# Per-row score maxima: turned by matmuls that read each column 64 times over, in place of a spread copy and a transpose

## The chip, the cores and the metric

The kernel runs on one core of a Trainium2 chip. The metric is the device time of one execution in microseconds (us). The engines are PE (TensorE, with its weight loads shown apart as PEld), DVE (VectorE), ACT (ScalarE), POOL (GpSimd) and SP (SyncE, which here only issues DMAs). Each runs its own list of instructions in order, and waits on semaphores for the others.

## The reference

One transformer block, float32, batch 2, 2048 positions, width 256, 16 heads of 64, hidden width 768:

```
hn = layernorm(h) * gamma + beta
q, k, v = hn @ Wq + bq, hn @ Wk + bk, hn @ Wv + bv      # 16 heads of 64
q, k = rope(q), rope(k)
attn = softmax(where(causal, q @ k.T * 64**-0.5, -inf))
x = layernorm(h + (attn @ v) @ Wo + bo + h)
out = layernorm(x + (silu(x @ Wg) * (x @ Wu)) @ Wd + x) # integer weights times 1/127
```

## The kernel before

The work on attention is cut into 16 pairs of heads (8 pairs for each of 2 batches; `it` counts them from 0). The two heads of a pair lie in the two halves of the 128 partitions (`halves`), 64 rows each. A pair has 16 query tiles of 128 rows and 4 blocks of 512 queries, and its scores are made transposed, keys on the partitions: 40 units of 128 keys by up to 512 queries (`UNITS`). Two units make a group, and every engine runs through the same 20 groups, `g` from 0 to 19, in the same order (`pair`, written once for each engine).

The softmax subtracts each row's maximum. The maxima are made ahead of the scores, from a coarser product: `maxima` on PE writes a query tile against up to 512 keys, for both heads, into the two banks of `m_ps`; `maximum` on DVE reduces it along the keys (L833) and, for tiles with several pieces, reduces the pieces once more (L836). So the negated maximum of query row p of tile t, head a, ends in `mc[p, block, t, a]`: one number per partition, a column. `m_ps` is not doubled: PE's next `maxima` waits until DVE has reduced the last.

The scores need these maxima along the free axis, on the partitions of the head's half, because they are added by one more product: `ones_r` (64 rows of ones) times `aux` (L1211) adds the sum over the half's 64 rows of `aux` to every score of a query. Before the change this goes in three steps. `spread` on DVE copies 8 columns of `mc` (4 tiles, 2 heads) into `mz`, a buffer of zeros, at column 0 and column 64 of each tile (L847). `turn_maxima` on PE transposes the four tiles of `mz` into `x_ps` (L1222), so that row 0 and row 64 hold the maxima and the other rows are zero. `shifts` on ACT copies `x_ps` to `aux` (L575).

There is one such turn for each block, called M0 to M3: M1 in group 1, M2 in group 5, M3 in group 11, and M0 of the next pair in group 19. The table `XUSE` has them, since the one bank `x_ps` is shared with the projections of the next pair's q and k ("Q0", "K0", ...), with v ("V0", ...) and with the row sums ("R0", ...). `shared_free` makes PE wait until the last user has left the bank: before M2 that is K0, before M3 it is Q2, and both are left by DVE (`products`: L860 writes `qr`, L864 writes `qc`). The rope needs the halves of `qr` swapped: SP issues four DMAs for it (L385, `rot<-qr`), and then DVE adds (`turned_sum`, L871); ACT rounds (L569) and DVE takes the rest (`piece_lo`, L876).

In a turn's group PE runs: one `maxima`; the scores of two units (L1205 to L1215); the turn; `weigh` of the group before (the probabilities times v, L1239). DVE runs: the copy (`spread`); the sums' transpose (group 1) or the two `products` (groups 5 and 11); the maximum of this group; then the rest. POOL adds up the probabilities (`acc`, L542) all the time.

L1239 and L1222 differ in how PE's array is cut. L1239 has 128 rows by 64 columns of weights, one half for each head, and the two halves run side by side; the trace shows each plain float32 product as two records. L1222 uses all 128 by 128, and a transpose is one record.

Of the kernel before, what the change touches and what calls it, by code (L numbers as in the profile page):

```python
# [8 lines left out]
F32 = mybir.dt.float32  # L9
# [4 lines left out]
P = 128  # L14
BATCH, SEQ, DM = 2, 2048, 256
HEADS, DK = 16, 64
# [3 lines left out]
TT = SEQ // P  # L20
# [3 lines left out]
TG = 4  # L24
GROUPS = TT // TG
NB = 512
BLOCKS = SEQ // NB
# [11 lines left out]
NM = len(MUNITS)  # L39
GU = 2  # L40
NG = NU // GU
# [21 lines left out]
TURN_M = {g: int(x[1]) for g, x in XUSE.items() if x[0] == "M"}  # L63
# [38 lines left out]
def postln_block_kernel(nc, h, gamma, beta, wqkv, bqk, bv, wo, bo, wgate_t, wup_t, wdown_t,  # L102
                        cos, sin, ident, masks, attn, hn_far, v_far, out):
    h, out = h.rearrange("b s d -> (b s) d"), out.rearrange("b s d -> (b s) d")
    with ExitStack() as ctx:
        def sb(name, shape, dt):
            return ctx.enter_context(nc.sbuf_tensor(name, shape, dt))

        def sem(name):
            return ctx.enter_context(nc.semaphore(name))  # L110
# [6 lines left out]
        id_f = sb("id_f", [P, P], F32)  # L117
        mask_b = sb("mask_b", [P, 4, P], BF16)
        id_b = sb("id_b", [P, DK], BF16)
        ones_r = sb("ones_r", [P, P], F32R)  # L120
# [6 lines left out]
        b_v = sb("b_v", [P, OC], F32)  # L127
        mz = sb("mz", [P, TG, P], F32)
        mc = sb("mc", [P, BLOCKS, TG, 2], F32)
# [77 lines left out]
        with ExitStack() as ctx_ps:  # L207
# [3 lines left out]
            x_ps = ctx_ps.enter_context(nc.psum_tensor("x_ps", [P, NB], F32))  # L211
# [48 lines left out]
        maxed = sem("maxed")  # L260
        m_rows = sem("m_rows")
        mz_done = sem("mz_done")
        m_turned = sem("m_turned")
# [10 lines left out]
        normed = sem("normed")  # L274
# [30 lines left out]
        out_stored = sem("out_stored")  # L305

        FIRST, MIDDLE, SWITCH, LAST = "first", "middle", "switch", "last"
# [472 lines left out]
        def _(dve):  # L780
            nc.vector.memset(mz[:, :, :], 0.0).then_inc(normed, 1)
            nc.vector.memset(ones_f[:, :], 1.0).then_inc(o_stored, 16)
            nc.vector.memset(ones_r[:, :].bitcast(F32), 1.0).then_inc(out_stored, 16)
            nc.vector.memset(r_i[:, :], 0.0).then_inc(tile_done, 1)
# [42 lines left out]
            def maximum(n, m):  # L827
# [6 lines left out]
                if parts > 1 and c == parts - 1:  # L834
                    dve.wait_ge(maxed, n * NM + (m + 1))
                    nc.vector.tensor_reduce(mc[:, t // TG, t % TG, :], mpart[:, t % 2, :, 0:parts],  # L836
                                            AX.X, ALU.min).then_inc(m_rows, 1)

            def spread(n, blk, first=False):

                if blk == 0:
                    dve.wait_ge(maxed, n * NM + TG)
                else:
                    dve.wait_ge(m_rows, n * (TT - TG) + TG * blk)
                if not first:
                    dve.wait_ge(m_turned, n * BLOCKS + blk)
                nc.vector.tensor_copy(mz[:, :, :].rearrange("p t (a d) -> p t a d", a=2)[:, :, :, 0], mc[:, blk, :, :])\  # L847
                  .then_inc(mz_done, 1)

# [60 lines left out]
            def pair(kind, it, par, pr, batch):  # L910
                for g in range(NG):
                    turns = g in TURN_M and (g != NG - 1 or kind is not LAST)
                    if turns and kind is not FIRST:
                        spread(it + 1 if g == NG - 1 else it, TURN_M[g])
                    ended = EVICTED.get(g) if g != 1 or kind is not FIRST else None
# [6 lines left out]
                    for m in ms[:late]:  # L922
                        maximum(it, m) if m < NM else maximum(it + 1, m - NM)
                    if turns and kind is FIRST:
                        spread(it + 1 if g == NG - 1 else it, TURN_M[g])
                    if g - 2 in PIECE and kind is not LAST:
# [81 lines left out]
            remainders(1)  # L1008
            spread(0, 0, first=True)
            unturned(3)  # L1010
# [126 lines left out]
        def _(pe):  # L1137
# [6 lines left out]
            halves = (slice(0, DK), slice(DK, P))  # L1144
# [74 lines left out]
            def turn_maxima(n, blk):  # L1219
                pe.wait_ge(mz_done, n * BLOCKS + (blk + 1))  # L1220
                for t in range(TG):
                    last = nc.tensor.transpose(x_ps[:, t * P:(t + 1) * P], mz[:, t, :], id_f[:, :])  # L1222
                last.then_inc(m_turned, 1)
# [254 lines left out]
```

## Time and profile before

| | us |
|---|---|
| median of 3 runs | 2232.11 (2231.62 to 2236.57) |
| profiled execution, its own time | 2229.82 |
| profiled execution, span | 2228.0 |
| PE busy | 2070.0 (93%) |
| DVE busy | 1597.6 (72%) |
| POOL busy | 1391.7 (62%) |
| ACT busy | 906.6 (41%) |

The busy times are unions over the span. The times in the rows further down count from the start of the span. The 16 pairs run from about 70 us to 1850 us; the input's normalization and first projections lie before, the output projection and the feed-forward part behind.

### The profile page before, as it was taken

How to read it: one execution, taken by the hardware profiler on the slowest of the kernel's cores; microseconds unless marked ns; L12 is line 12 of the kernel's file. 1: busy time of each engine (PE TensorE's matmuls, PEld its weight loads, DVE VectorE, ACT ScalarE, POOL GpSimd, SP SyncE). 2: the span in 40 equal slices, each digit the busy share in tenths (PEclk: the TensorE clock that was granted, in tenths of full speed). 3: DMA queues.
4: the chain of work that ended last, by engine and by line, in shares of the span. 5: the costliest groups of instructions: out<-in, count | busy, mean ns of one | idle time of the engine just before them, and what ended most of it. 6: DMA issues, size and time to landing. Idle time of an engine off the chain costs nothing.

```text
span 2228.0 us, 37497 instructions
## 1 busy us (share of the span) xinstructions
PE 2070.0 (93%) x14720; PEld 1287.2 (58%) x14720; DVE 1597.6 (72%) x2262; ACT 906.6 (41%) x1245; POOL 1391.7 (62%) x1204
## 2 busy tenths in 40 slices
PE   6779999999999989999999999999999989889997
PEld 5445555555555545555555555555555545789996
DVE  8576878686878776767777777778787763556654
ACT  4424443444444434434343434343434345434342
POOL 1457777777787866677767777878787879000000
PEclk9899999999999999999999999999999999999999
DMA  6311212121202122122111212121112131231300
GB/s 223 119 30 38 62 39 62 39 62 39 58 25 68 42 68 72 45 65 63 48 53 43 58 43 58 43 58 34 48 34 58 29 119 48 67 104 57 112 10 29
DMA packets 116149, 132.16 MB, mean 59 GB/s; under 512 B 15248, under 2 KB 71184, under 8 KB 115728
## 3 DMA queue, kind: packets, MB, share of 16 engines
q1 hardware_dynamic: 115984, 129.92, 19.5%
q8 instruction: 109, 1.79, 0.3%
q14 instruction: 56, 0.46, 0.1%
HBM read 56.47 MB, written 39.85 MB: 43 GB/s over the span
## 4 chain that ended last, share of the span: by engine, by line
PE 60%; DVE 24%; DMA 5%; SPq 4%; issue 4%; ACT 1%; POOL 1%; ACTq 0%; DVEq 0%
PE o_ps L1239 13%; DVE mpart L833 9%; PE m_ps L1184 7%; DMA rot<-qr 5%; PE s_ps L1205 4%; SPq L385 4%; PE s_ps L1209 4%; PE s_ps L1207 4%; PE s_ps L1211 4%; PE x_ps L1139 3%; DVE qr L860 3%; PE x_ps L1246 3%; DVE qc L871 2%; PE gu_ps L1139 2%; PE gu_ps L1140 2%
## 5 line engine op out<-in xcount | busy, mean ns | idle before, releaser
L542 POOL TENSOR_TENSOR acc<-acc,pt 128x512 f32<-128x512 f32 (+3 forms) x1024 | 1195.8, 1200 | 228.0 <-ACT pt L591 228.0
L591 ACT ACTIVATE pt<-s_ps 128x1024 f32<-128x1024 f32 (+3 forms) x640 | 544.8, 895 | 704.8 <-PE s_ps L1211 342.4
L833 DVE TENSOR_REDUCE mpart<-m_ps 128x2 f32<-128x1024 f32 (+2 forms) x576 | 624.9, 1085 | 288.2 <-PE m_ps L1184 215.7
L1239 PE MATMUL o_ps<-pt,v 128*64 128x512 f32 (+3 forms) x2560 | 547.5, 549 | 0.0
L1184 PE MATMUL m_ps<-qk 64*128 64x512 f32 (+3 forms) x1280 | 290.0, 449 | 85.0 <-DVE mpart L833 73.7
L1184 PEld LDWEIGHTS m_ps<-qk 64*128 64x128 f32 x1280 | 121.1, 185 | 395.6 <-DVE mpart L833 223.6
L1239 PEld LDWEIGHTS o_ps<-pt,v 128*64 128x64 f32 x2560 | 157.8, 138 | 239.1 <-issue 213.8
L537 POOL TENSOR_TENSOR acc<-pt 128x512 f32<-128x512 f32 (+1 forms) x128 | 161.7, 1283 | 193.7 <-ACT pt L591 193.7
L1205 PE MATMUL s_ps<-qk 64*128 64x512 f32 (+3 forms) x1280 | 253.7, 392 | 0.0
L1209 PE MATMUL s_ps<-qk 64*128 64x512 f32 (+3 forms) x1280 | 235.6, 363 | 0.0
L1211 PE MATMUL s_ps<-aux,ones_r 64*128 64x512 f32 (+3 forms) x1280 | 234.7, 362 | 0.0
L1207 PE MATMUL s_ps<-qk 64*128 64x512 f32 (+3 forms) x1280 | 234.3, 362 | 0.0
L871 DVE TENSOR_TENSOR qc<-qc,rot 128x512 f32<-128x512 f32 x128 | 139.6, 1091 | 113.4 <-DMA rot<-qr 113.3
L569 ACT ACTIVATE qk<-qc 128x512 fp32r<-128x512 f32 x128 | 80.0, 629 | 253.2 <-DVE qc L871 253.2
L876 DVE TENSOR_TENSOR qk<-qc,qk 128x512 fp32r<-128x512 f32 x128 | 140.8, 1103 | 0.2 <-ACT qk L569 0.2
L1209 PEld LDWEIGHTS s_ps<-qk 64*128 64x128 f32 x1280 | 121.2, 185 | 20.3
L1211 PEld LDWEIGHTS s_ps<-aux,ones_r 64*128 64x128 f32 x1280 | 121.5, 185 | 19.1
L1207 PEld LDWEIGHTS s_ps<-qk 64*128 64x128 f32 x1280 | 122.1, 187 | 16.5
L1205 PEld LDWEIGHTS s_ps<-qk 64*128 64x128 f32 x1280 | 122.1, 187 | 15.8 <-ACT pt L591 4.9
L1139 PE MATMUL x_ps<-hn,w_hl 128*128 128x512 f32 x240 | 107.7, 449 | 0.0
L1141 PE MATMUL x_ps<-hn,w_hl 128*128 128x512 f32 x240 | 95.3, 397 | 0.0
L1140 PE MATMUL x_ps<-hn,w_hl 128*128 128x512 f32 x240 | 95.1, 396 | 0.0
(165 smaller groups left out, 2882.0 us busy)
## 6 DMA issues: line engine op xcount, KB each, us to landing
rot<-qr SPq DMA_DIRECT2D x512, 64.0 KB, 2.0
attn<-o_sum SPq DMA_DIRECT2D x64, 256.0 KB, 2.3
o_raw<-attn SPq DMA_DIRECT2D x8, 2048.0 KB, 8.9
v<-v_far SPq DMA_DIRECT2D x16, 768.0 KB, 5.2
v_far<-v_part SPq DMA_DIRECT2D x48, 256.0 KB, 2.0
w_raw<-in_wqkv SPq DMA_DIRECT2D x34, 128.0 KB, 5.1
v_far<-v SPq DMA_DIRECT2D x16, 256.0 KB, 2.4
v<-v_far SPq DMA_DIRECT2D x16, 256.0 KB, 5.0
```

The source lines that it names most:

```text
L537: last = nc.gpsimd.tensor_tensor(sums, pt[:, (u - 1) % SLOTS, a, q0:NB], probs, ALU.add)
L542: nc.gpsimd.tensor_tensor(sums, sums, probs, ALU.add).then_inc(summed, 1)
L591: nc.scalar.activation(pt[:, u % SLOTS, :, q0:NB], s_ps[:, two:two + 2, q0:NB], ACT.Exp, scale=SCALE)\
L833: nc.vector.tensor_reduce(dst, m_ps[:, :, 0:w], AX.X, ALU.max, negate=True).then_inc(maxed, 1)
L871: nc.vector.tensor_tensor(qc[:, c % 2, a, :], qc[:, c % 2, a, :], rot[:, a, :], ALU.add).then_inc(roped, 1)
L1139: nc.tensor.matmul(dst, lhs[0], rhs[0], start=first, stop=False)
L1184: last = nc.tensor.matmul(m_ps[:, a, 0:w], qk[par][rows, 0, q], qk[par][rows, 1, k], start=True, stop=not diag)
L1205: nc.tensor.matmul(dst[a], qk[par][rows, 1, k], qk[par][rows, 0, q], start=True, stop=False)
L1207: nc.tensor.matmul(dst[a], qk[par][rows, 1, k], qk[par][rows, 2, q], start=False, stop=False)
L1209: nc.tensor.matmul(dst[a], qk[par][rows, 3, k], qk[par][rows, 0, q], start=False, stop=False)
L1211: last = nc.tensor.matmul(dst[a], ones_r[rows, :], aux[rows, q0:NB], start=False, stop=not diag)
L1239: last = nc.tensor.matmul(o_ps[rows, q0:NB], v[par][:, j, rows], pt[:, u % SLOTS, a, q0:NB], start=(j == 0), stop=(j == n - 1), skip_group ...
```

## The change

`spread`, its buffer `mz` and its semaphore go. PE takes the maxima from `mc` itself, for each tile and head with one float32 product with the identity: its weights are the column `mc[:, blk, t, a:a+1]`, read 64 times over by an access pattern of step 0, 128 rows by 64 columns, and its moving operand is the identity, 128 columns. So all 64 rows of the head's half of `x_ps` hold the maxima, not one row. `ones_r` becomes 1/64 to make up for it. PE now waits for the reductions (`maxed`, `m_rows`) where it waited for the copy. `mc` is cleared at the start in place of `mz`.

```diff
-            nc.vector.memset(mz[:, :, :], 0.0).then_inc(normed, 1)
             nc.vector.memset(ones_f[:, :], 1.0).then_inc(o_stored, 16)
-            nc.vector.memset(ones_r[:, :].bitcast(F32), 1.0).then_inc(out_stored, 16)
+            nc.vector.memset(ones_r[:, :].bitcast(F32), 1.0 / DK).then_inc(out_stored, 16)
+            nc.vector.memset(mc[:, :, :, :], 0.0).then_inc(normed, 1)
...
-            def spread(n, blk, first=False):
-
-                if blk == 0:
-                    dve.wait_ge(maxed, n * NM + TG)
-                else:
-                    dve.wait_ge(m_rows, n * (TT - TG) + TG * blk)
-                if not first:
-                    dve.wait_ge(m_turned, n * BLOCKS + blk)
-                nc.vector.tensor_copy(mz[:, :, :].rearrange("p t (a d) -> p t a d", a=2)[:, :, :, 0], mc[:, blk, :, :])\
-                  .then_inc(mz_done, 1)
...
-                    turns = g in TURN_M and (g != NG - 1 or kind is not LAST)
-                    if turns and kind is not FIRST:
-                        spread(it + 1 if g == NG - 1 else it, TURN_M[g])
...
             def turn_maxima(n, blk):
-                pe.wait_ge(mz_done, n * BLOCKS + (blk + 1))
+
+                if blk == 0:
+                    pe.wait_ge(maxed, n * NM + TG)
+                else:
+                    pe.wait_ge(m_rows, n * (TT - TG) + TG * blk)
                 for t in range(TG):
-                    last = nc.tensor.transpose(x_ps[:, t * P:(t + 1) * P], mz[:, t, :], id_f[:, :])
+                    for a, rows in enumerate(halves):
+                        last = nc.tensor.matmul(x_ps[rows, t * P:(t + 1) * P], mc[:, blk, t, a:a + 1].broadcast_to([P, DK]),
+                                                id_f[:, :], start=True, stop=True, skip_group_check=True)
                 last.then_inc(m_turned, 1)
```

Two places show how the order on the engines moves. The first is DVE around M2 of pair 4 (group 5), before the change:

```order
L871 TENSOR_TENSOR qc<-qc,rot 128x512
L847 COPY mz<-mc 128x8
L860 SCALAR_TENSOR_TENSOR qr<-x_ps,b_qk,sin_sb 128x512
L864 SCALAR_TENSOR_TENSOR qc<-x_ps,b_qk,cos_sb 128x512
L833 TENSOR_REDUCE mpart<-m_ps 128x2
```

and the same place in the changed kernel:

```order
L858 TENSOR_TENSOR qc<-qc,rot 128x512
L847 SCALAR_TENSOR_TENSOR qr<-x_ps,b_qk,sin_sb 128x512
L851 SCALAR_TENSOR_TENSOR qc<-x_ps,b_qk,cos_sb 128x512
L831 TENSOR_REDUCE mpart<-m_ps 128x2
L863 TENSOR_TENSOR qk<-qc,qk 128x512
```

The copy is gone, and the products that empty `x_ps` stand directly behind the rope's addition; line numbers are lower because code has gone, and nothing else has moved. The second place is PE at the same turn, before (each of the rows is a number of instructions of the program, output partitions by columns):

```order
L1211 MATMUL s_ps<-aux,ones_r 128x128 x2
L1215 MATMUL s_ps<-id_b,mask_b 128x64 x4
L1222 MATMUL x_ps<-id_f,mz 128x128 x4
L1239 MATMUL o_ps<-pt,v 64x512 x2
L1239 MATMUL o_ps<-pt,v 64x384 x2
```

and in the changed kernel:

```order
L1192 MATMUL s_ps<-aux,ones_r 128x128 x2
L1196 MATMUL s_ps<-id_b,mask_b 128x64 x4
L1208 MATMUL x_ps<-id_f,mc 64x128 x8
L1226 MATMUL o_ps<-pt,v 64x512 x2
L1226 MATMUL o_ps<-pt,v 64x384 x2
```

Four full-width transposes have become eight half-width products, in the place where the four stood, ahead of products of the same half-width kind.

## Rows read from the trace of the kernel before

**Rows 1.** The page's first lines: span and busy times.

```profile
span 2228.0 us, 37497 instructions
PE 2070.0 (93%) x14720; PEld 1287.2 (58%) x14720; DVE 1597.6 (72%) x2262; ACT 906.6 (41%) x1245; POOL 1391.7 (62%) x1204
```

**Rows 2.** Groups of instructions: shapes, count | busy, mean ns | idle before, releaser.

```profile
L1184 PE MATMUL m_ps<-qk 64*128 64x512 f32 (+3 forms) x1280 | 290.0, 449 | 85.0 <-DVE mpart L833 73.7 <-DVE mc L833 6.4 <-DVE qc L864 1.2
...
L847 DVE COPY mz<-mc 128x8 f32<-128x8 f32 x64 | 56.5, 882 | 0.1
...
L1222 PE MATMUL x_ps<-id_f,mz 128*128 128x128 f32 x256 | 42.7, 290 | 13.9 <-DVE qc L864 10.1 <-DVE mz L847 3.6
```

**Rows 3.** Lines L847 and L1222 alone: durations; idle PE and PEld (us, times).

```profile
L847 DVE COPY mz<-mc x64: 166/968/1253, 55.7 to 1848.0; 128x8 f32<-128x8 f32 x64
...
  DVE qc L864: 23.3, 52
```

**Rows 4.** Chain that ended last: its first and last piece on L847.

```profile
88.20 0.19 DVE mz L847
...
1740.13 0.89 DVE mz L847
```

**Rows 5.** Timeline of DVE at M2 of pair 4: start, us, instruction [idle before].

```profile
577.96 1.48 DVE L871 TENSOR_TENSOR qc<-qc,rot 128x512 f32<-128x512 f32 x1 [1.74 <-DMA rot<-qr]
579.37 0.98 DVE L847 COPY mz<-mc 128x8 f32<-128x8 f32 x1
580.26 0.74 DVE L860 SCALAR_TENSOR_TENSOR qr<-x_ps,b_qk,sin_sb 128x512 f32<-128x512 f32 x1
...
584.84 0.69 DVE L871 TENSOR_TENSOR qc<-qc,rot 128x512 f32<-128x512 f32 x1 [1.28 <-DMA rot<-qr]
585.45 1.22 DVE L833 TENSOR_REDUCE mpart<-m_ps 128x2 f32<-128x1024 f32 x1
```

**Rows 6.** Timeline of POOL at the same place: four additions in one row.

```profile
575.43 4.88 POOL L542 TENSOR_TENSOR acc<-acc,pt 128x512 f32<-128x512 f32 x4 [1.54 <-ACT pt L591]
```

**Rows 7.** Timeline of PE at the same place.

```profile
581.71 0.66 PE L1222 MATMUL x_ps<-id_f,mz 128*128 128x128 f32 x4 [1.17 <-DVE qc L864]
...
585.91 0.40 PE L1211 MATMUL s_ps<-aux,ones_r 64*128 64x512 f32 x2
586.72 0.49 PE L1184 MATMUL m_ps<-qk 64*128 64x512 f32 x2 [0.41 <-DVE mpart L833]
```

**Rows 8.** Timeline, PE and PEld: half-width products, two passes of 256, two of 128 columns.

```profile
510.64 0.87 PE L1239 MATMUL o_ps<-pt,v 128*64 128x256 f32 x8
511.34 1.03 PE L1246 MATMUL x_ps<-acc,ones_f 128*64 128x512 f32 x4
...
511.13 0.14 PEld L1239 LDWEIGHTS o_ps<-pt,v 128*64 128x64 f32 x2
511.24 0.14 PEld L1246 LDWEIGHTS x_ps<-acc,ones_f 128*64 128x64 f32 x2
```

**Rows 9.** Timeline of PE at an M0 (group 19 of pair 3).

```profile
550.92 0.24 PE L1215 MATMUL s_ps<-id_b,mask_b 64*128 64x64 bf16 x4
551.09 0.66 PE L1222 MATMUL x_ps<-id_f,mz 128*128 128x128 f32 x4
551.67 1.08 PE L1239 MATMUL o_ps<-pt,v 128*64 128x512 f32 x4
```

**Rows 10.** Timeline of PE at M2 of pair 11, and its next wait.

```profile
1382.23 0.66 PE L1222 MATMUL x_ps<-id_f,mz 128*128 128x128 f32 x4 [0.23 <-DVE qc L864]
...
1387.30 0.50 PE L1184 MATMUL m_ps<-qk 64*128 64x512 f32 x2 [0.47 <-DVE mpart L833]
```

**Rows 11.** Timeline of PE at M3 of pair 10, and its next wait.

```profile
1306.05 0.66 PE L1222 MATMUL x_ps<-id_f,mz 128*128 128x128 f32 x4 [0.32 <-DVE qc L864]
...
1311.65 0.44 PE L1184 MATMUL m_ps<-qk 64*128 64x384 f32 x2 [0.96 <-DVE mc L833]
```

**Rows 12.** Timeline of PE at M1 of pair 0.

```profile
88.52 1.09 PE L1222 MATMUL x_ps<-id_f,mz 128*128 128x128 f32 x4 [1.82 <-DVE mz L847]
```

More of the change, by code:

```diff
@@ L127, in postln_block_kernel @@
         b_v = sb("b_v", [P, OC], F32)
-        mz = sb("mz", [P, TG, P], F32)
         mc = sb("mc", [P, BLOCKS, TG, 2], F32)
@@ L261, in postln_block_kernel @@
         m_rows = sem("m_rows")
-        mz_done = sem("mz_done")
         m_turned = sem("m_turned")
@@ L923, in pair @@
                         maximum(it, m) if m < NM else maximum(it + 1, m - NM)
-                    if turns and kind is FIRST:
-                        spread(it + 1 if g == NG - 1 else it, TURN_M[g])
                     if g - 2 in PIECE and kind is not LAST:
@@ L1008, in _ @@
             remainders(1)
-            spread(0, 0, first=True)
             unturned(3)
```

## Prediction

> **What bounds the kernel now.** I read the page first, then the groups, then the two lines that the change touches, then the chain that ended last, and last the timelines around several turns. PE is busy for 93% of the span, DVE for 72%, POOL for 62% [rows 1]. That makes PE the bound, but not all the way: PE's idle time before `maxima` is 85.0 us, and 73.7 us of it is a wait for DVE's reduction L833 [rows 2]. So in most places PE's own work sets the pace, and in some places DVE, whose next reduction is late because other work stands ahead of it. The change moves work between just these two: off DVE, onto PE. Its worth is read turn by turn, from whether PE waits behind the turn.
>
> The copy is dear for its size. Eight numbers per partition take 166 ns at best, but 968 ns in the median [rows 3], 56.5 us in all [rows 2]. The copy of pair 4 ends at 580.35, just as a stretch of POOL additions ends at 580.31 [rows 5, 6]: it seems to wait for POOL, not to compute.
>
> The chain that ended last tells where those copies matter. It runs over 28 of the 64, from the one at 88.20 to the one at 1740.13 [rows 4]: 2 of pair 0, otherwise only M2 and M3, never M0 or M1. Summed over its pieces that is 24.6 us. At M2 one sees why: the copy lies between the rope's addition and L860 [rows 5], L860 feeds both `x_ps`, which PE waits for (idle 1.17 us), and the swap by DMA, whose end at 584.84 lets DVE do L871 and then L833, for which PE waits again (0.41 us) [rows 5, 7]. At M0 the turn starts with no wait at all [rows 9]: a copy there costs nobody anything.
>
> **What the change costs on PE.** Before, from the first transpose to the first product behind it: 551.09 to 551.67, 0.58 us [rows 9]. After, there are 8 program products, 16 records, in 8 passes, since the two halves run side by side. The nearest row is the same shape, half-width weights with 128 moving columns: its weight loads come as a pair at 511.13 and the next pair at 511.24, 0.11 us per pass [rows 8]. As a check, the whole stretch from 510.64 to 511.34 is 0.70 us for two passes of 256 and two of 128 columns: 0.43 + 0.22 = 0.65, and 0.05 for the first load, which nothing hides [rows 8]. So the new turn takes 0.05 + 8 x 0.11 = 0.93 us. `weigh` behind it has the same shape, and saves its own first 0.05. Net: 0.93 - 0.58 - 0.05 = **+0.30 us** of PE per turn. The lower bound is 0 (the passes could not beat the transposes' 0.58 by any row), the upper is 16 loads one behind another (below). I take 0.30, because the row is of the very shape.
>
> The Trainium skill ("TensorEngine Tiling (Array Packing)", Key Properties) says that changing the tiling mode drains TensorE. By it alone the old turn, full width between two tiled kinds, paid two drains and the new one pays one; it gives no price. The rows above already hold it: the 0.05 at entry, and what the old 0.58 holds beyond four passes of 0.11, 0.14 us.
>
> **What it gives back on DVE.** The copy's slot runs from its start at 579.37 to L860's at 580.26: 0.89 us less 0.01; I use 0.88 [rows 5]. No operation is added on DVE (the memset of `mc` is smaller than that of `mz`, and both lie before the inputs have landed). PE's wait is now for the reduction itself, which ends before the copy starts.
>
> PE gains at a turn the smaller of two: the 0.88 by which DVE is earlier, or its own stalls there less the 0.30. The stall is more than the idle time shown, since a record's end runs over the next start. Without a wait a turn starts 0.07 before the scores' end (550.92 + 0.24 against 551.09) [rows 9], so 0.07 is to be added. `maxima` without a wait would follow L1211 after 0.23, one step of such products, at 586.14, and came at 586.72: 0.58, where 0.41 is shown, so 0.17 is to be added [rows 7].
>
> Going through the 64 turns by kind:
> - M0 and M1 of pairs 1 to 15, 30 turns. PE does not wait there [rows 9]: +9.0.
> - Two M2 and two M3 (pairs 6, 7 and 15) without a wait: +1.2.
> - Pair 0: two turns at full clock, +0.6. M1 and M2 run at half speed (1.09 us where others take 0.66 [rows 12, 9]), so they cost +0.6 each, and here PE waits for the copy directly (1.82 idle [rows 12]), which gives back about 0.3 each. Together +1.2.
> - 9 M2 with long stalls (like pair 4: 1.17 + 0.07 + 0.58 = 1.82; after the cost 1.52 is left): DVE's 0.88 is the smaller, -7.9.
> - 4 M2 with short stalls (like pair 11: 0.23 + 0.07 + 0.47 + 0.17 = 0.94 [rows 10]): about 0.90 on average, less 0.30: -2.4.
> - 3 M3 with a long second stall (like pair 10: 0.32 + 0.07 + 0.96 + 0.17 = 1.52 [rows 11]): -2.6. One in between: -0.5.
> - 9 M3 where only the first stall is there, 0.24 to 0.35 shown, so about 0.37: less 0.30, -0.6 together.
>
> Costs 11.4, gains 14.0: **-2.6 us**, call it -3. Written with the cost c of a turn open, the same list is about 52 c - 18.9 (all turns count but the 12 long ones), so 0.05 us more or less per turn is 2.6 us. So 24.6 us leave the chain, yet most of it doesn't reach the end: where DVE stops being late, PE is late next, 0.3 later than before. Stalls differ a little from turn to turn, so the list carries an error of some 2 us.
>
> **Sum.** The profiled execution took 2229.82 us; less 3 gives 2226.8. The median of the runs is 2.3 above that execution, so I expect a median of **2229.0**. What a measurement can tell from no change is about 0.2%, 4.5 us, and my -3 lies inside.
>
> **What else could happen.**
> *The lead adds up.* If DVE's 0.88 at the short turns isn't lost but carried to later stalls of PE (85.0 us of idle before `maxima` in all), the whole 24.6 comes back against costs of 11.4: -13.2, 2218.9. For it: the waits for L833 are many. Against: DVE, having reduced, waits for PE's next product in many places too, and there a lead ends.
>
> *The loads don't overlap (slower).* If the weights of one pass can't load while the pass before streams, in one column group of the array, the 16 loads stand one behind another; at 0.11 each (the step between loads is all that the rows give) a turn takes 1.76 + 0.05, so +1.18 net, not +0.30. The point from which it decides is +0.36 per turn, where 52 c passes 18.9. At +1.18 it is 61 - 19, and the long turns lose some 3 of their gain: +45, 2275. Against: the load at 511.24 belongs to the pass that starts at 511.34, so it ran under the pass before [rows 8]. The Trainium skill ("TensorE: Matmul & The Clock Gate", Part 3, The mechanism) speaks against the change here: it says that a weight load overlaps a running matmul only when its row group is another one, and all of these have the same rows. The rows disagree with it for this shape. What no row shows is such a load read with step 0.
>
> *Other operations of DVE fall differently against POOL's.* L871 takes 1.48 us at 577.96 and 0.69 at 584.84, where POOL is idle [rows 5, 6]: it waits for POOL's additions just as the copy did. With the copy gone, DVE's two-input operations start elsewhere in POOL's rhythm, and may win or lose up to some 0.4 us each at a place on the chain. One such per pair is 16 x 0.4 = 6 us either way: 2223 to 2235. It decides the sign from 0.2 us lost per pair. The Trainium skill ("SBUF — State Buffer", Who interferes with whom) says that a copy in a two-port mode and a GpSimd operation exclude each other for the whole instruction, and that an operation with two SBUF inputs contends with GpSimd's reads too; the rows fit both.
>
> *The copy was no real cost* (removed where DVE would have been idle anyway): true at M0, excluded at M2 by the chain [rows 4].
>
> **How the numbers follow.** The forecast's case: 0.52 (of it 0.38 within 0.2%, 0.14 just faster than that, as its error of 2 us allows). The lead adds up: 0.15, faster. Loads in a row: 0.08, slower. POOL's rhythm: 0.25 (0.12 slower, 0.10 same, 0.03 faster). That gives 0.32 faster, 0.48 the same, 0.20 slower. Range for 8 in 10: the low end 2221 takes in the forecast's error and part of the first rival, the high end 2238 takes in POOL's rhythm at its worst and the spread of the runs, but not the loads in a row.
>
> **What would show it.** The new products: 16 records per turn, 0.11 between passes, and 0.93 from the first to `weigh`. DVE busy 56 us less. At M2 and M3 the turn's idle before it gone; the waits for L833 behind M2 shorter, those elsewhere as now; PE's busy time up by about 19. From the turn M0 to the turn M1 0.3 us more. The prediction is wrong if a turn takes over 1.1 us, if idle time before `maxima` falls by over 15 us, or if L871, L876 or the division change their mean by over 0.1 us.

## The result and the profile after

The changed kernel takes 2211.81 us in the median of 4 runs (2208.03 to 2215.79), the kernel before 2231.86 (4 runs, 2229.92 to 2236.57): ratio 0.9913, 95% interval 0.9888 to 0.9938. That is 20 us or 0.9% faster, outside my range, where I forecast 3 us. The profiled execution took 2210.01 us, 19.8 less than that of before. The page's first lines, after:

```profile
span 2208.1 us, 38906 instructions
...
PE 2076.2 (94%) x15488; PEld 1315.9 (60%) x15488; DVE 1552.8 (70%) x2198; ACT 908.5 (41%) x1245; POOL 1397.6 (63%) x1204
```

DVE has 44.8 us less to do (56.5 for the copy, but its record of 0.98 us filled a slot of 0.89 [rows 5], which is 6 us over 64, and L863 and L858 take 4.6 longer), and PE 6.2 more where I expected 19. The groups of instructions after, `weigh` (L1226), `maxima` (L1165), the turn (L1208) and DVE's remainders (L863):

```profile
L1226 PE MATMUL o_ps<-pt,v 128*64 128x512 f32 (+3 forms) x2560 | 538.4, 541 | 0.0
L1165 PE MATMUL m_ps<-qk 64*128 64x512 f32 (+3 forms) x1280 | 288.2, 446 | 69.8 <-DVE mpart L831 62.1
...
L863 DVE TENSOR_TENSOR qk<-qc,qk 128x512 fp32r<-128x512 f32 x128 | 144.8, 1134 | 0.3 <-ACT qk L567 0.3
```

```profile
L1208 PE MATMUL x_ps<-id_f,mc 128*64 128x128 f32 x1024 | 71.7, 283 | 4.8 <-DVE mc L834 3.2 <-DVE qc L851 1.5
```

and `weigh` before, which the change doesn't touch:

```profile
L1239 PE MATMUL o_ps<-pt,v 128*64 128x512 f32 (+3 forms) x2560 | 547.5, 549 | 0.0
```

Against [rows 2], PE's idle time before `maxima` falls from 85.0 to 69.8 us and that before the turn from 13.9 to 4.8. What I had not looked for is in `weigh`: the same 2560 records take 541 ns instead of 549 in the mean, and their busy time, in which records side by side count once, is 9.1 us less. 2.7 us of that aren't the clock. They are the 0.05 per turn that my sum has: behind the new turn the first product's two records take 592 ns at full clock, behind the old one 643 (the x4 of [rows 9] takes 1.08 us, the one below 1.03). The other 6.5 us are the clock: the traces show `weigh` losing 10.1 us to the low clock before and 3.6 after.

The turn itself is as forecast. The timeline of PE at M0 of the same pair as [rows 9]:

```profile
552.63 0.23 PE L1196 MATMUL s_ps<-id_b,mask_b 64*128 64x64 bf16 x4
552.80 1.09 PE L1208 MATMUL x_ps<-id_f,mc 128*64 128x128 f32 x16
553.72 1.03 PE L1226 MATMUL o_ps<-pt,v 128*64 128x512 f32 x4
```

From the first product to `weigh` 0.92 us (0.93 forecast, 0.58 before). The rule of the Trainium skill that spoke against the change ("TensorE: Matmul & The Clock Gate", Part 3, The mechanism: a load overlaps a matmul only if its row group differs) doesn't hold for this shape: 16 records, all on the same rows and read with step 0, in 0.92 us. The same section also names a second way, a load into the background weight buffer; which of the two applies here no row shows. The timeline at M2 of pair 4, DVE and PE, beside [rows 5, 7]:

```profile
573.26 0.74 DVE L847 SCALAR_TENSOR_TENSOR qr<-x_ps,b_qk,sin_sb 128x512 f32<-128x512 f32 x1
...
574.71 1.09 PE L1208 MATMUL x_ps<-id_f,mc 128*64 128x128 f32 x16 [0.30 <-DVE qc L851]
...
577.85 0.69 DVE L858 TENSOR_TENSOR qc<-qc,rot 128x512 f32<-128x512 f32 x1 [1.23 <-DMA rot<-qr]
578.45 1.22 DVE L831 TENSOR_REDUCE mpart<-m_ps 128x2 f32<-128x1024 f32 x1
```

The stall ahead of the turn is 0.30, where it was 1.17. It is the copy's 0.88 and no more: the next things to be late are the swap and L858, as before.

**The clock.** PE's clock has two levels, 2.4 GHz and half of it. The stretches from turn to turn of pair 0, before (start and end, us, PE's busy time and its records, granted clock as a share of full, the DMA engines' share and GB/s):

```profile
62.50:88.50 26.00, 15.32 (x117) 0.72 0.46 152
88.50:122.00 33.50, 25.19 (x172) 0.91 0.29 80
122.00:167.90 45.90, 38.22 (x247) 0.93 0.09 26
```

and after:

```profile
63.00:88.70 25.70, 16.04 (x129) 0.72 0.45 152
88.70:121.30 32.60, 24.49 (x186) 0.92 0.29 82
121.30:166.50 45.20, 37.53 (x260) 0.95 0.09 27
```

The same for the stretch from M2 to M3 of pair 6, before and after, with PE's waits in it:

```profile
794.05 0.66 PE L1222 MATMUL x_ps<-id_f,mz 128*128 128x128 f32 x4 [0.23 <-DVE qc L864]
799.05 0.51 PE L1184 MATMUL m_ps<-qk 64*128 64x512 f32 x2 [0.40 <-DVE mpart L833]
812.84 0.49 PE L1184 MATMUL m_ps<-qk 64*128 64x512 f32 x2 [3.08 <-DVE mpart L833]
832.82 0.47 PE L1139 MATMUL x_ps<-wv_hl,hn 128*128 128x512 f32 x1 [1.88 <-issue]
```

```profile
794.00:835.90 41.90, 36.48 (x239) 0.96 0.23 63
```

```profile
806.00 0.49 PE L1165 MATMUL m_ps<-qk 64*128 64x512 f32 x2 [3.05 <-DVE mpart L831]
823.55 0.47 PE L1120 MATMUL x_ps<-wv_hl,hn 128*128 128x512 f32 x1 [1.03 <-issue]
```

```profile
787.50:826.60 39.10, 35.02 (x255) 1.00 0.24 67
```

Before, PE ran part of this stretch at the low clock, behind a wait of 3.08 us; after, the wait of 3.05 is still there, the small ones ahead of it are gone, and the clock stays up. The stretch takes 39.1 instead of 41.9 us. Of these 2.8 us, 1.7 are the clock and 1.5 PE's waits (the last one, of 1.88, is 1.03), and the turn costs 0.3. The Trainium skill ("TensorE: Matmul & The Clock Gate", Part 1) says that the clock follows how busy PE has been recently. This stretch doesn't show that the small waits decide it: two kernels of the table below, e4 and e7, are the changed kernel at another position, have the same two waits (3.04 and 1.03, 3.02 and 1.00) and no others, and yet lose 1.7 and 3.4 us to the low clock in it, while e18 has small waits too (0.30 and 0.81, ahead of 3.03) and none of it at the low clock.

Every run, not only the profiled one, comes with its span and its mean granted clock. Below, "clock loss" is span x (1 - clock): what PE would save at full clock if it never idled, so an upper estimate. Over 92 runs of the kernel before (19 to 23 beside each group of experiments, 11 beside the last), it varies from 38 to 58 us, and the span follows it with a correlation of 0.85 and a slope of 0.77 us per us. The rest, span less loss, scatters by only 2.2 us, and is the sharper measure of what a kernel's instructions cost.

### The profile page after: what moved, and what is told of

Read it like the earlier page. It is cut to its first block, busy times and chain, and to the rows that moved or that the text cites. A ratio compares the mean times of both kernels' runs of the same rounds, so it can differ in the third digit from the quotient of the medians.

```text
span 2208.1 us, 38906 instructions
## 1 busy us (share of the span) xinstructions
PE 2076.2 (94%) x15488; PEld 1315.9 (60%) x15488; DVE 1552.8 (70%) x2198; ACT 908.5 (41%) x1245; POOL 1397.6 (63%) x1204
## 3 DMA queue, kind: packets, MB, share of 16 engines
q8 instruction: 115, 1.88, 0.4%
## 4 chain that ended last, share of the span: by engine, by line
PE 67%; DVE 21%; DMA 4%; issue 3%; SPq 3%; ACT 1%; POOL 1%; ACTq 0%; DVEq 0%
PE o_ps L1226 15%; DVE mpart L831 8%; PE m_ps L1165 8%; PE s_ps L1186 5%; PE s_ps L1190 4%; PE s_ps L1188 4%; PE s_ps L1192 4%; DMA rot<-qr 3%; PE x_ps L1120 3%; SPq L383 3%; PE x_ps L1208 3%; DVE qc L858 3%; PE x_ps L1233 2%; PE x_ps L1122 2%; PE x_ps L1121 2%
## 5 line engine op out<-in xcount | busy, mean ns | idle before, releaser
L1226 PE MATMUL o_ps<-pt,v 128*64 128x512 f32 (+3 forms) x2560 | 538.4, 541 | 0.0
L1165 PE MATMUL m_ps<-qk 64*128 64x512 f32 (+3 forms) x1280 | 288.2, 446 | 69.8 <-DVE mpart L831 62.1
L1165 PEld LDWEIGHTS m_ps<-qk 64*128 64x128 f32 x1280 | 120.8, 185 | 372.8 <-DVE mpart L831 215.4
L1226 PEld LDWEIGHTS o_ps<-pt,v 128*64 128x64 f32 x2560 | 159.7, 137 | 224.4 <-issue 204.2
L535 POOL TENSOR_TENSOR acc<-pt 128x512 f32<-128x512 f32 (+1 forms) x128 | 166.6, 1323 | 173.9 <-ACT pt L589 173.9
L858 DVE TENSOR_TENSOR qc<-qc,rot 128x512 f32<-128x512 f32 x128 | 140.2, 1096 | 105.9 <-DMA rot<-qr 105.8
L863 DVE TENSOR_TENSOR qk<-qc,qk 128x512 fp32r<-128x512 f32 x128 | 144.8, 1134 | 0.3 <-ACT qk L567 0.3
L1188 PEld LDWEIGHTS s_ps<-qk 64*128 64x128 f32 x1280 | 122.3, 187 | 16.4
L1186 PEld LDWEIGHTS s_ps<-qk 64*128 64x128 f32 x1280 | 122.2, 187 | 15.7 <-ACT pt L589 4.9
```

Of the source, the lines that this page charges most:

```text
L535: last = nc.gpsimd.tensor_tensor(sums, pt[:, (u - 1) % SLOTS, a, q0:NB], probs, ALU.add)
L858: nc.vector.tensor_tensor(qc[:, c % 2, a, :], qc[:, c % 2, a, :], rot[:, a, :], ALU.add).then_inc(roped, 1)
L1165: last = nc.tensor.matmul(m_ps[:, a, 0:w], qk[par][rows, 0, q], qk[par][rows, 1, k], start=True, stop=not diag)
L1186: nc.tensor.matmul(dst[a], qk[par][rows, 1, k], qk[par][rows, 0, q], start=True, stop=False)
L1188: nc.tensor.matmul(dst[a], qk[par][rows, 1, k], qk[par][rows, 2, q], start=False, stop=False)
L1226: last = nc.tensor.matmul(o_ps[rows, q0:NB], v[par][:, j, rows], pt[:, u % SLOTS, a, q0:NB], start=(j == 0), stop=(j == n - 1), skip_group ...
```

## The experiments

All 18 in one table. Time is the median of the timed runs. Span, loss and rest are means over each kernel's runs (4 to 12; 92 for the kernel before). "Idle" is PE's idle time before `maxima` plus that before the turn, from the groups of the one profiled execution (before: 85.0 + 13.9).

| kernel | time | ratio [95%] | span | loss | rest | idle |
|---|---|---|---|---|---|---|
| before | 2227.9 to 2230.2 in five groups | | 2227.4 | 48.7 | 2178.6 | 98.9 |
| e5 before, shifted 32 | 2230.5 | 1.0003 [0.9981, 1.0025] | 2228.2 | 50.1 | 2178.1 | 102.1 |
| e3 before, shifted 64 | 2234.0 | 1.0027 [1.0012, 1.0042] | 2232.5 | 47.6 | 2185.0 | 103.9 |
| e6 before, shifted 128 | 2223.4 | 0.9979 [0.9966, 0.9992] | 2222.2 | 45.3 | 2176.9 | 96.8 |
| e13 before, SyncE waits | 2232.6 | 1.0014 [1.0, 1.0028] | 2230.4 | 49.3 | 2181.2 | 96.7 |
| after | 2211.8 | 0.9913 [0.9888, 0.9938] | 2210.0 | 38.1 | 2171.9 | 74.6 |
| e4 after, shifted 64 | 2208.8 | 0.9905 [0.9888, 0.9921] | 2207.5 | 35.9 | 2171.6 | 76.0 |
| e7 after, shifted 128 | 2214.9 | 0.9932 [0.9908, 0.9957] | 2212.6 | 40.4 | 2172.2 | 76.6 |
| e14 after, SyncE waits | 2219.0 | 0.9952 [0.9929, 0.9975] | 2216.3 | 41.7 | 2174.6 | 76.5 |
| e1 dead copy | 2229.1 | 0.9996 [0.9985, 1.0008] | 2227.2 | 42.3 | 2184.9 | 83.5 |
| e9 dead copy, shifted 128 | 2227.3 | 0.9987 [0.9972, 1.0001] | 2225.5 | 39.1 | 2186.4 | 86.9 |
| e15 dead copy, SyncE waits | 2228.1 | 0.9997 [0.9983, 1.001] | 2227.4 | 41.2 | 2186.2 | 85.8 |
| e2 direct | 2199.8 | 0.987 [0.9838, 0.9902] | 2198.3 | 44.5 | 2153.8 | 75.8 |
| e8 direct, shifted 64 | 2199.9 | 0.9881 [0.9845, 0.9917] | 2200.2 | 41.8 | 2158.4 | 81.9 |
| e12 direct, shifted 128 | 2202.0 | 0.987 [0.985, 0.989] | 2199.7 | 41.4 | 2158.3 | 79.8 |
| e16 direct, SyncE waits | 2203.6 | 0.9884 [0.9859, 0.9909] | 2201.6 | 45.7 | 2155.9 | 74.2 |
| e10 new turn at M2, M3 | 2207.3 | 0.9895 [0.9877, 0.9913] | 2205.2 | 42.3 | 2163.0 | 78.8 |
| e11 new turn at M0, M1 | 2230.6 | 1.0006 [0.9991, 1.0022] | 2229.4 | 41.8 | 2187.6 | 98.0 |
| e17 before, swaps held | 2259.3 | 1.0135 [1.0111, 1.0159] | 2256.8 | 51.2 | 2205.7 | 121.8 |
| e18 after, swaps held | 2240.4 | 1.0058 [1.0035, 1.0081] | 2238.6 | 42.9 | 2195.7 | 95.5 |

**Copy or turn: the dead copy and the direct kernel.** In e1 the copy is still made, and nobody waits for it (the lines that call it; `mz` and `spread` come back too):

```diff
                 for g in range(NG):
+                    turns = g in TURN_M and (g != NG - 1 or kind is not LAST)
+                    if turns and kind is not FIRST:
+                        spread(it + 1 if g == NG - 1 else it, TURN_M[g])
```

> The changed kernel with the copy into mz still made on DVE, in its old place, though nobody waits for it. Theory A (fetches): the trace of before has 18 of 128 rope swaps that land after about 3.5 us in place of 2.0, each with a 16 KB instruction packet on queue 8 beside it, and the changed kernel's other count of PE instructions moved these away from the places where PE waits; that gave some 16 of the 20 us, the copy the rest. Then this kernel, with the changed kernel's PE stream, keeps most of the 16: before plus 34 turns x 0.3 = 2242, less 16, so about 2226. Theory B (the lead adds up: DVE's relief is worth more than counted at each turn): the copy back means the whole relief gone and the cost of the turns kept: about 2242, slower than before.

In e2 the reductions write straight into a spread buffer, three of them in turn, and PE makes the four transposes of before; no copy, and not the new turn:

```diff
-        mz = sb("mz", [P, TG, P], F32)
+        mz = sb("mz", [P, 3, TG, P], F32)
...
-                dst = mc[:, t // TG, t % TG, :] if parts == 1 else mpart[:, t % 2, :, c]
+                dst = mz[:, (n * BLOCKS + t // TG) % 3, t % TG, 0:P:DK] if parts == 1 else mpart[:, t % 2, :, c]
```

> DVE's reductions write straight into a spread buffer (three of them in rotation) and PE transposes it as before: no copy, and no dearer turn. PE's stream has before's instruction count, so also its fetches. Turn 0.58 us from first transpose to weigh in both theories. By my list with c = 0 the gain against before is 18.9 us. Theory A: about 2213 (the slow swaps of before's count stay, though shifted in time). Theory B: the changed kernel's 2211.8 less 52 x 0.3, so about 2196.

With the copy back the gain is gone (2229.1). Theory A had 2226 for e1 and 2213 for e2, theory B 2242 and 2196: the first number lies near A's and the second near B's, so neither holds as it stands. Without copy and with the old turn the kernel is 12 us faster again than the changed one (2199.8), so the new turn costs 12 us in time and 16 in the rest (2172.6 against 2156.6, means over four kernels each). My list said 52 x 0.30 = 15.6. The groups of the turn in e2, and of turn and copy in e1:

```profile
L1209 PE MATMUL x_ps<-id_f,mz 128*128 128x128 f32 x256 | 42.8, 291 | 4.8 <-DVE mz L836 3.2 <-DVE qc L853 1.6
```

```profile
L1227 PE MATMUL x_ps<-id_f,mc 128*64 128x128 f32 x1024 | 72.6, 286 | 13.6 <-DVE qc L864 10.4 <-DVE mc L836 3.2
...
L847 DVE COPY mz<-mc 128x8 f32<-128x8 f32 x64 | 55.7, 871 | 0.1
```

The idle time before the turn is 4.8 without the copy and 13.6 with it, whichever turn it is: that wait is the copy's. A longer turn, on the other hand, takes up stalls by itself: with the copy kept, the idle time falls from 99.7 (mean of the five kernels of before's kind) to 85.4 us in the three dead-copy ones.

**Is it an accident of position?** PE's instructions arrive in packets, and some swaps land late beside one (last section). So both kernels were run again with PE's stream moved on by 32 to 128 instructions, with long-met waits ahead of pair 0. Two such waits make one instruction, so the 128 of e3 and e4 shift by 64, as the table has it, and not by the 128 of their names:

```diff
             pe.wait_ge(primed, 1)
+            for _ in range(128):
+                pe.wait_ge(primed, 1)
```

> The kernel before, with 128 extra waits on PE that are long met, put where PE idles at the start: half the 256 instructions that lie between two 16 KB fetches, and no other work. Theory A: other swaps are hit, and the time moves by several us, either way; since before seems unlucky, likely to 2218 to 2228. Theory B: within 2 us of before, 2230 to 2234.

> The same 128 waits in the changed kernel. Theory A: moves by several us, likely up, 2214 to 2226, since its own count seems lucky. Theory B: 2210 to 2214. The number of swaps that land after more than 2.5 us (14 in the changed kernel) and which of them precede M2 and M3 should change in both shifted kernels.

> The kernel before with its PE stream shifted by 32 instructions (the first shift, of 128 waits, had proved to be 64 instructions: two waits go into one). Theory A now claims less: the edit itself is worth what undisturbed pairs show, and each kernel carries a sum of late swaps that depends on where its PE stream meets the 16 KB fetches. Before has 9 late swaps on its chain (13.7 us above 2 us each), shifted by 64 it has 13 (21.6 us) and takes 3.7 us more. Theory A expects here again another set of late swaps, and time following their sum on the chain at 0.5 to 1 us per us: if it falls to 5 us, some 2223 to 2227. Theory B: 2230 to 2234 whatever the swaps.

> Shifted by 128 instructions, half the distance between two fetches. Theory A: as above, other swaps late than in before and its shift by 64; the time follows their sum on the chain. Theory B: within 2 us of before.

> The changed kernel shifted by 128. It has 5.0 us of late swaps on its chain, shifted by 64 it has 5.6. Theory A (chance): with a third phase the sum can as well be 10 to 15 us, and the time 2215 to 2220. Theory C (the copy's absence makes the chain less exposed to late swaps, since DVE is 0.9 us earlier at each): the sum on the chain stays at about 5 whatever the phase, and the time at 2208 to 2213.

> The kernel without copy and without dearer turns, shifted by 64. It has 4.8 us of late swaps on the chain with the PE stream of before, which has 13.7 there. Theory A: may go to 10 or more, time up to 2205. Theory C: stays near 5, time within 3 us of 2199.8.

Position moves a kernel by some 4 us either way (the one of before from 2223.4 to 2234.0) and doesn't change the order of the three. Theory B, which wanted the kernel before to stay within 2 us, missed e3 and e6 (+3.7 and -4.5 against the kernel before of their groups), and e4 and e7 (2208.8 and 2214.9) fell outside every range that was set for them. In the mean over five kernels of before's kind and four of after's, the spans are 2228.1 and 2211.6: -16.6 us, of which the clock loss has -9.2 (48.2 to 39.0) and the rest -7.4 (2180.0 to 2172.6).

**Which turns pay.** e10 has the new turn at M2 and M3 and keeps copy and transposes at M0 and M1; e11 is the complement; each takes the other form by block, with a second constant of 1/64 beside the ones:

```diff
+                if blk in (2, 3):
+                    for t in range(TG):
+                        for a, rows in enumerate(halves):
+                            last = nc.tensor.matmul(x_ps[rows, t * P:(t + 1) * P], mc[:, blk, t, a:a + 1].broadcast_to([P, DK]),
...
+                else:
+                    pe.wait_ge(mz_done, 2 * n + {0: 1, 1: 2}[blk])
```

> The changed kernel with the copy still made on DVE, unused, as in the first run of it, but with PE's instruction stream 128 instructions further on (256 long-met waits ahead of pair 0, where PE idles), so that PE's instruction packets meet other swaps. Theory 1 (the dearer turn costs 0.3 us each at M0 and M1, and the first dead-copy kernel hid this behind few late swaps, 10 with 4.2 us of excess on the chain where the kernel before has 15.2 on average): the time is 2229.6 + 10 less what its late swaps save against the 15.2 on the chain, 2232 to 2242. Theory 2 (the turn costs nothing once PE need not wait for the copy): 2229 again, 2226 to 2231. Segments from turn M0 to turn M1: 8.41 us under theory 1 in any case.

> The new turn at M2 and M3 alone; at M0 and M1 the copy on DVE and the four transposes stay. Theory 1 (the copy's slot is worth something only where PE waits behind DVE, at M2 and M3; the dearer turn costs 0.3 at M0 and M1): all of the change's gain without its 4.4 us of cost from M0 to M1 and the like at M1: M0 to M1 8.13 us as before, 4 to 9 us faster than the changed kernel, 2203 to 2208. Theory 2 (the lead adds up, each copy that goes is worth the same): half of the gain, about 2220.

> The complement: the new turn at M0 and M1 alone; at M2 and M3 the copy and the transposes stay. Theory 1: only the cost, 30 x 0.3 = 9 us and none of the gain: 2234 to 2240, with M0 to M1 at 8.41 us and about 15 us of late swaps' excess on the chain. Theory 2 (each copy that goes is worth the same): about 2220.

> The kernel in which DVE's reductions write straight into three rotating spread buffers and PE makes the four transposes as before, with PE's instruction stream 128 instructions further on. Theory 1 (its gain is no accident of which swaps meet an instruction packet): 2196 to 2204, like the 2199.8 and 2199.9 at the two other positions. The rival, that both were lucky positions: 2208 or more.

All of the gain is at M2 and M3: e10 is 22 us faster than before and 4.5 faster than the full change; e11 is level with before in time. Theory 1's 2234 to 2240 for e11 was too high all the same, and its rest shows why: 9.0 above before, just the 30 x 0.30 of the list, but its clock loss is 6.9 lower. The three dead-copy kernels tell the same: their rest is 7 above before's, their loss 8 below, and the time comes out level. For e9 that is theory 2's number, but not for its reason, since the dearer turn is there in the rest. So the dearer turn is partly paid by the clock.

The stretches from turn to turn show it without the clock. They come from the starts of the turns in the timelines (M0 to M1 of pair 4: 559.22 - 551.09 before, 552.80 - 544.39 after), less the clock loss in each; medians over pairs 1 to 15 and over the kernels of one kind:

| | M0 to M1 | M1 to M2 |
|---|---|---|
| before | 8.13 | 21.56 |
| after | 8.41 | 21.55 |
| new turn at M2, M3 | 8.12 | 21.27 |
| new turn at M0, M1 | 8.41 | 21.86 |
| direct | 8.13 | 21.27 |

A new turn adds 0.28 to 0.30 us where PE doesn't wait; no copy at M2 gives back 0.29 in the stretch that ends there. M2 to M3 falls from 35.12 to 34.14 and is 34.09 in the direct kernel: there the new turn costs almost nothing beside the old one, as it should where DVE sets the pace. M3 to M0 goes from 45.41 to 45.55.

**Late swaps.** A theory that I held for a while: part of the gain comes from swaps that land late, which a DVE without the copy can take up. The next four kernels were to delay every swap with 24 waits on SyncE:

```diff
                 sp.wait_ge(qk_raw, done)
+                for _ in range(24):
+                    sp.wait_ge(primed, 1)
```

> The kernel before, with every swap issued later: 24 waits on a semaphore long met on SyncE ahead of its four DMAs, an estimated 1.0 to 1.5 us. Theory 1 (with the copy in DVE's way at M2 and M3 there is no slack there: a late swap costs over 1 us in the stretch from M2 to M3 and 0.9 in the one to M0, as the late ones did): with 28 such stretches that are not late now, 15 to 40 us slower than the kernel before. Theory 2 (late swaps cost both kernels the same, and the changed one was lucky): slower by the same amount as the changed kernel with the same delay.

> The changed kernel with every swap issued later in the same way. Theory 1 (DVE has the copy's 0.9 us to take it up; a late swap cost it 0 to 0.2 us): 0 to 15 us slower than the changed kernel, and its lead over the kernel before grows from 18 us to 30 or more. Theory 2: the lead stays at 6 to 18 us.

> The changed kernel with the copy still made and unused, every swap issued later in the same way. Theory 1: as slow as the kernel before with late swaps, plus up to the 9 us of its dearer turns. The rival (it is the longer turn of PE that covers a late swap, not the copy's absence): clearly faster than the kernel before with late swaps, by 8 us or more.

> Reductions straight into the spread buffers, four transposes, no copy, every swap issued later in the same way. Theory 1: 10 us faster than the changed kernel with late swaps, as without them, since both have the copy's slot free. The rival (the longer turn covers the late swap): level with it, or slower.

These did not do what they were made for: from the end of `qr` to the first of the swap's DMAs it is 0.03 us in the median, as without the waits, and only four swaps ahead of pair 0 were issued later (by 0.6 to 1.4 us). They say nothing on the theory and stand in the table as further positions. The delay that works holds each swap until the cosine product behind the sine product is made:

```diff
                 sp.wait_ge(qk_raw, done)
+                sp.wait_ge(cos_done, done)
```

> The kernel before, with every swap held until DVE has also made the cosine product behind the sine product that the swap reads: 0.66 to 0.74 us later, all 128 of them. Theory 1 (at M2 and M3 the copy leaves no slack for a late swap): a swap late by 1.5 us cost 1.4 us in the stretch from M2 to M3 and 0.7 in the one from M3 to M0, so in proportion 0.7 us cost about 15 x 0.65 + 14 x 0.33 = 14 us: 8 to 22 us slower than the kernel before. Theory 2 (what differed between the two kernels was which swaps were late): as much slower as the changed kernel with the same delay, within 4 us.

> The changed kernel with every swap held in the same way. Theory 1 (the copy's 0.88 us is free to take up 0.7 us): a swap late by 1.5 us cost it 0 to 0.2 us, so 0 to 5 us slower than the changed kernel, and its lead over the kernel before grows by 8 us or more. Theory 2: as much slower as the kernel before with the same delay, within 4 us.

The timeline of DVE and of SyncE's queue in e17 shows the hold: the swap leaves after the second product, 0.73 us later.

```profile
578.78 0.73 DVE L861 SCALAR_TENSOR_TENSOR qr<-x_ps,b_qk,sin_sb 128x512 f32<-128x512 f32 x1
579.44 0.73 DVE L865 SCALAR_TENSOR_TENSOR qc<-x_ps,b_qk,cos_sb 128x512 f32<-128x512 f32 x1
580.25 2.42 SPq L386 DMA_DIRECT2D rot<-qr  x4
```

0.73 us at 128 swaps costs the kernel before 31 us and the changed one 28.6, and the lead is 18.9 us, about as without it (ratio of the two 0.9917). Theory 2 gave this within 4 us; theory 1 had 8 to 22 us for the kernel before, 0 to 5 for the changed one and a lead that grows by 8 or more, and misses all three. The copy's absence isn't worth more when all swaps are late.

## Why the prediction was wrong

**What held.** The turn (0.92 for 0.93), the overlap of the loads, +0.28 from M0 to M1 for +0.3, no cost for the load of step 0 (137 ns in the median, as the loads of `weigh`), DVE's busy time (down 44.8 of 56: L863 has gone from 1103 to 1134 ns, L858 from 1091 to 1096, under the 0.1 that I had set), and the gain at M2 and M3 only.

**What failed** are two terms of the sum. The plainer one is "PE's busy time up by about 19". It rose by 9.3 (2070.9 to 2080.2, means over the five and four kernels). I had taken every duration of PE as the one profile had it, and added new work at full clock: the clock had no term. I had read the low clock of pair 0 ("M1 and M2 run at half speed") as a property of the place, but it changes from kernel to kernel. Each trace gives PE's busy time and the part of it that the low clock added. That part fell by 5.9 us (38.7 to 32.8), 2.6 of it in `weigh`.

The busy time without it rose by 15.1 (2032.3 to 2047.4), and that isn't the turn's fault. The four direct kernels have the old turn and no copy, and 2028.4: beside them the new turn adds 19.0, as forecast. The direct kernels run the same products as the kernel before, with 3.9 us less of busy time at full clock. I read that as the ends of records that show only where PE stalls, my 0.07 and 0.17.

The second term is the gains. Their 14.0 are net of the 0.30 at 26 turns with a stall (9 + 4 + 3 + 1 + 9), so PE's stalls, these ends included, were to fall by 14.0 + 7.8 = 21.8. The idle time fell by 23.8 (99.7 to 75.9), with the 3.9 it is 27.7. So the list had -21.8 + 19.2 = -2.6, and the profiled runs show -27.7 + 19.0, -5.9 for the clock and -1.4 elsewhere, together -15.9 of span but for rounding. The clock and the mis-sized gains have 5.9 each of the 13.3 us between them.

The granted clock of all runs gives the same picture from the other side: the loss is 9.2 us lower, the rest 7.4. With the slope of 0.77 the clock is worth 7 us or so, at most 9. The profiled stretches tell where it falls: in pair 0 the loss is 10.2 to 11.9 us in the nine kernels that have the new turn at M0 and M1, and 13.7 to 20.5 in the eleven that haven't, so there it comes with the new turn; that the longer turn does it by filling PE's time is argued. In pairs 1 to 15, it varies more, from 5.1 to 13.7 in the four kernels of after's kind and from 10.2 to 13.7 in the five of before's (means 10.2 and 11.9), too wide for a difference of 1.7 to be read as the change's. Why the clock goes up is open: no kernel changed the clock alone, and pair 6 speaks against the small waits as the only cause.

**The rest**, -7.4 for -2.6, is mis-sized by 5 us, more than the 2 of error that I gave the list. The other kernels miss it alike: the direct one has -23.4 against before's mean where the list has -18.9, e10 about -17 where it has -12, while e11, which keeps the copy at M2 and M3, fits (+7.6 to +9.0 for +9). So what is too small is the worth of a copy at M2 or M3, by some 0.15 us each. Compared stretch by stretch, without the clock, pairs 1 to 15 take 1620.4 us before and 1609.5 after, and nearly all of that difference lies in stretches in which a swap was late (landed over 2.5 us after the issue of its last DMA). The stretches without a late swap, pair by pair, add up to 0.5 us less after, for the 3.8 that the list has for these pairs. From M2 to M3 a late swap cost 1.1 us before and 0.3 after, against the same pair's stretches without one (24 late of 75, and 20 of 60); and the kernels of before's kind have more of them, 18 against 14.5 in the mean. At pair 2 both kernels have a late swap behind M2, so it can be read. Before:

```profile
353.36 0.50 PE L1184 MATMUL m_ps<-qk 64*128 64x512 f32 x2
...
355.20 0.66 PE L1222 MATMUL x_ps<-id_f,mz 128*128 128x128 f32 x4 [0.23 <-DVE qc L864]
...
359.78 0.69 DVE L871 TENSOR_TENSOR qc<-qc,rot 128x512 f32<-128x512 f32 x1 [2.61 <-DMA rot<-qr]
360.39 1.22 DVE L833 TENSOR_REDUCE mpart<-m_ps 128x2 f32<-128x1024 f32 x1
...
361.66 0.50 PE L1184 MATMUL m_ps<-qk 64*128 64x512 f32 x2 [1.86 <-DVE mpart L833]
```

After:

```profile
353.07 0.50 PE L1165 MATMUL m_ps<-qk 64*128 64x512 f32 x2
...
354.61 1.09 PE L1208 MATMUL x_ps<-id_f,mc 128*64 128x128 f32 x16
...
358.18 0.69 DVE L858 TENSOR_TENSOR qc<-qc,rot 128x512 f32<-128x512 f32 x1 [1.98 <-DMA rot<-qr]
...
360.06 0.50 PE L1165 MATMUL m_ps<-qk 64*128 64x512 f32 x2 [0.57 <-DVE mpart L831]
```

1.86 of idle time is 0.57 here. From the `maxima` ahead of the turn to the one behind the stall it is 8.30 us before and 6.99 after, 1.31 less. The two swaps aren't equally late (3.43 and 3.00 us after the issue of the last DMA), which has 0.43 of that; 0.88 is left, the copy's slot. So a late swap makes a long stall of a short one, and then the full 0.88 comes back where I had booked 0.6 net at such a turn. But the kernels with all swaps held don't bear out that this makes the lead larger, so how much of the 5 us it explains stays open, as does why a late swap cost only 0.5 us in that stretch of the dead-copy kernels, which have the copy (11 stretches of 45).

**The rivals.** "The lead adds up" named 2218.9, the nearest of my numbers. It wanted PE's stalls to fall by 24.6 + 7.8 = 32.4, and they fell by 27.7, between it and the list; in the median M1 to M2 and M3 to M0 gained nothing, so there no lead was carried on. "Loads in a row" is refuted. "POOL's rhythm" stayed small (L863 +31 ns, 4 us of DVE's time). I had set a fall of more than 15 us in the idle time before `maxima` as a sign of error; it was 15.2 in the one profile and 14.0 in the means of the kernels. No rival had the clock.

**The best kernel** of the study is the direct one, 26 to 30 us below the kernel before in its four groups. It needs neither the copy nor the new turn. The new turn's one merit beside it is the clock in pair 0 (loss 13.7 to 15.4 us for 10.2 to 11.9); a direct kernel with the new turn in pair 0 alone was not run.

## What to carry to other kernels

Don't price PE's work at the clock of one profile when a change moves PE's waits: take span x (1 - clock) from every run, compare that and the rest apart, and give the clock a term and a rival of its own. A copy between two engines is dear by what stands behind it in the queue, not by its size: here 32 of 64 copies held all of the gain. And where the writer can put the data where the reader wants it at no price, that beats making the reader do the spreading: the last reduction of a row (L836) takes 159 ns in the kernel before and 161 in the direct one, where its output is strided.

## What was not expected of the hardware

The swaps' lateness comes with PE's instruction stream. The DMA queues in the window of 353 to 362 us, before, where the swap behind M2 of pair 2 is late:

```profile
q1 hardware_dynamic: 192, 0.26, 12.1%
q8 instruction: 1, 0.02, 0.8%
```

Packets of 16 KB come on q8, 109 in the kernel before and 115 after. PE has 1536 records more after, loads and products, so that is one packet per 256. Of the 22 swaps with such a packet that starts between 1.5 us before and 1.9 us after the issue of the last DMA, 18 landed over 2.5 us after it (2.8 to 3.8 where 2.0 is usual); of the 106 others none. After it is 14 of 17, and none of 111. The bounds were drawn on these traces; in the other 18 kernels the same ones give 262 of 377, and 8 of 1927. Which swaps they meet changes with every instruction that is added to PE's stream ahead of them, as the late swaps of the shifted kernels show: 16, 26 and 14 in e5, e3 and e6, for 18.

The second is the size of the clock's part: in a kernel with PE 93% busy, the low clock still takes 38 to 58 us, as an upper estimate, of a run of one and the same program. In the profiles of before's five it is 16.4 in pair 0, 11.9 in the 15 other pairs, 15.7 behind them and 3.4 ahead (means). Those 20 us between runs are as much as this change brings, and they go with most of the scatter of the times.
